# Two transformer layers with experts on one core: the transfer of the maxima's rows moved to ScalarE's queue, rounds of 31 and 23 blocks, and another build-time order

## The reference, cut to what matters

```
xn = layernorm(x)
x  = x + attention0(xn) + (routed0(xn) + shared(xn))     # layer 0
xn = layernorm(x)
x  = x + attention1(xn) + routed1(xn)                    # layer 1
```

## Time and profile before

| | |
|---|---|
| median of 3 runs | 691.94 us (689.86 to 697.47) |
| the profiled execution's own time | 687.82 us |
| its span, first to last instruction | 686.0 us |
| mean granted PE clock in it | 0.973 |
| PE, PEld, DVE busy | 643.7, 352.8, 502.2 us |
| ACT, POOL busy | 450.7, 308.7 us |

### The profile page before, as it was taken

How to read it: one execution, slowest core, us unless ns; L and a number is a source line. 1 busy time by engine, 2 the same in 40 slices (tenths; PEclk the granted TensorE clock), 3 DMA queues, 4 the chain that set the end, 5 groups by cost and what they waited for, 6 DMA issues and landing times.

```text
span 686.0 us, 13133 instructions
## 1 busy us (share of the span) xinstructions
PE 643.7 (94%) x4200; PEld 352.8 (51%) x4200; DVE 502.2 (73%) x1088; ACT 450.7 (66%) x843; POOL 308.7 (45%) x422
## 2 busy tenths in 40 slices
PE   2999987999999999898999999899999999999986
PEld 1876742654544454333466566555656555656221
DVE  3699779787778798777858777876677777666732
ACT  2443258777768878565877676666667667666774
POOL 3256844873155635646482122666365122122550
PEclk9999998999999999799999999899999999999997
DMA  8954216365344434336645444444755554431110
GB/s 232 295 151 146 84 50 184 118 202 158 103 134 135 149 118 127 102 90 197 212 118 175 146 152 132 145 144 141 219 182 164 161 164 134 140 93 37 47 48 16
DMA packets 82965, 95.16 MB, mean 139 GB/s; under 512 B 7249, under 2 KB 70097, under 8 KB 82897
## 3 DMA queue, kind: packets, MB, share of 16 engines
q1 hardware_dynamic: 78800, 85.91, 41.7%
q0 software_dynamic: 4096, 8.40, 4.2%
HBM read 67.68 MB, written 26.21 MB: 137 GB/s over the span
## 4 chain that ended last, share of the span: by engine, by line
PE 75%; DVE 9%; issue 4%; DMA 3%; POOL 3%; ACT 3%; SPq 2%; another core or an unknown queue 1%; POOLq 0%; DVEq 0%; ACTq 0%
PE pv_ps L917 15%; PE slot L888 15%; PE slot L905 13%; PE slot L865 9%; PE slot L878 6%; PE pv_ps L779 5%; DVE mx L1285 3%; PE slot L854 2%; PE slot L925 2%; PE slot L847 2%; DMA wbuf<-in_experts 1%; PE slot L790 1%; PE slot L897 1%; ACT probsT L1047 1%
## 5 line engine op out<-in xcount | busy, mean ns | idle before, releaser
L1285 DVE TENSOR_REDUCE mx<-slot 128x1 f32<-128x512 f32 x512 | 334.9, 685 | 117.7 <-PE slot L888 94.3
L1047 ACT ACTIVATE probsT<-slot 128x512 f32<-128x512 f32 x512 | 284.2, 597 | 90.4 <-PE slot L905 71.7
L888 PE MATMUL slot<-k_stack,q_stack 72*128 72x512 bf16 x512 | 197.9, 387 | 9.6 <-DVE mx L1285 7.9
L905 PE MATMUL slot<-q_stack,k_stack 75*128 75x512 bf16 x512 | 194.6, 390 | 9.4 <-issue 3.6
L917 PE MATMUL pv_ps<-probsT,v 128*32 128x512 f32 x1024 | 140.5, 621 | 0.9 <-ACT probsT L1047 0.8
L1379 POOL TENSOR_TENSOR hid<-th,up 128x512 f32<-128x512 f32 (+2 forms) x56 | 71.2, 1271 | 130.5 <-DVE th L1148 76.6
L888 PEld LDWEIGHTS slot<-k_stack,q_stack 72*128 72x128 bf16 x512 | 50.1, 98 | 131.8 <-issue 74.7
L1367 POOL DMA_INDIRECT yg<-ys_hbm,index x64 | 62.2, 972 | 45.5 <-issue 34.1
L865 PEld LDWEIGHTS slot<-xgT,wbuf 128*128 128x128 f32 (+1 forms) x576 | 75.6, 186 | 12.3 <-issue 1.1
L905 PEld LDWEIGHTS slot<-q_stack,k_stack 75*128 75x128 bf16 x512 | 50.2, 99 | 58.0 <-issue 19.0
L1356 POOL DMA_INDIRECT xs_hbm<-xn,index x64 | 64.0, 1000 | 32.4 <-DVE index L1262 16.4
(11 more groups left out here) (133 smaller groups left out, 605.5 us busy)
## 6 DMA issues: line engine op xcount, KB each, us to landing
wbuf<-in_experts SPq DMA_DIRECT2D x48, 544.0 KB, 4.9
q_stack<-parts_hbm SPq DMA_DIRECT2D x96, 96.0 KB
k_stack<-parts_hbm SPq DMA_DIRECT2D x96, 96.0 KB
wbuf<-in_experts SPq DMA_DIRECT2D x64, 128.0 KB, 2.7
xg<-xs_hbm SPq DMA_DIRECT2D x28, 256.0 KB
ys_hbm<-ys SPq DMA_DIRECT2D x28, 256.0 KB, 2.6
parts_hbm<-parts SPq DMA_DIRECT2D x16, 384.0 KB
xs_hbm<-zeros SPq DMA_DIRECT2D x2, 2048.0 KB, 12.6
```

The costliest lines, as they stand in the source:

```text
L888: nc.tensor.matmul(ps[:, 0:N], q_stack[0:STACK, h, j * P:(j + 1) * P], k_stack[0:STACK, h, :], start=True, stop=True).then_inc(slot_full, 1)
L905: nc.tensor.matmul(ps[:, 0:N], k_stack[0:STACK + MAXROWS, h, j * P:(j + 1) * P], q_stack[:, h, :], start=True, stop=True).then_inc(slot_fu ...
L1047: nc.scalar.activation(probsT[:, k % PROBS, a, :], ps[:, 0:N], ACT.Exp, scale=SCALE).then_inc(slot_free, 1)
L1285: nc.vector.tensor_reduce(mx[:, g, u // J, u % J:u % J + 1], ps[:, 0:N], AXIS.X, ALU.max)\
```

## The change

1. The DMA of the maxima's rows is no longer a part of SP's list. A new stage NW, on ACT, waits for ACT's own copy to `mxT` and issues the same DMA from ACT's queue. It has the wanted moment of NT, and the planner books 0.75 us of ACT for it.
2. A round has 31 and 23 blocks in place of 32 and 24. The last group of each round then has three blocks: `live(r, q)` says how many, and every stage of the group is cut to that many blocks of 128 columns.
3. Nearly all wanted moments are others, WARM goes from 196 to 169, and `EDGE` shifts the moments of M, MP, NT and of E, PV of eleven single groups.

```diff
-NB = (32, 24)
+NB = (31, 23)
...
-SETUP = (2.045, -9.522, 8.07, 1.095, -8.469, -2.988, -1.684, 25.862)
-ROUTE = (0.046, 0.046, 31.138, 28.95)
-WEIGH = 0.485
-GROUPS = ((4.838, 0.586), (17.79, 0.521), (16.756, 0.924), (29.504, 0.606))
-SLACK = 0.253
-LAG = {'RF': (2.324, -1.184), 'M': (-1.1, -0.238), 'MP': (0.506, 0.56), 'NT': (0.625, -0.823), 'E': (1.07, 3.793), 'PV': (0.552, 0.573), 'PO': (4.67, 1.118), 'AT': (23.765, 0.84), 'WL': (-0.359, -0.605), 'XL': (-0.911, 0.582), 'GG': (-0.389, 5.152), 'DN': (0.742, -0.665), 'YS': (0.607, -1.125), 'YG': (-0.253, 1.108), 'RK': (0.014, 2.373), 'SL': (-1.025, 0.721), 'HI': (17.634, 0.832), 'PW': (5.769, -0.579)}
-WARM = 196
...
+SETUP = (-0.46, -1.532, 5.793, 3.492, -23.822, 0.878, 1.105, 12.168)
+ROUTE = (0.886, 14.043, 38.797, 27.291)
+WEIGH = -0.398
+GROUPS = ((12.343, 0.126), (22.692, 0.887), (31.727, 4.574), (54.836, 0.664))
+SLACK = 0.345
+LAG = {'RF': (23.695, -0.259), 'M': (-21.601, -4.266), 'MP': (-0.425, 1.142), 'NT': (0.685, 0.935), 'E': (7.873, 0.784), 'PV': (0.501, 1.616), 'PO': (-1.379, -0.462), 'AT': (21.887, 9.677), 'WL': (-18.538, -1.787), 'XL': (1.939, 0.99), 'GG': (2.258, 0.12), 'DN': (1.136, 0.696), 'YS': (0.671, -2.158), 'YG': (-6.421, 0.417), 'RK': (-14.371, 21.752), 'SL': (-21.114, 15.903), 'HI': (11.067, 0.945), 'PW': (0.847, 0.172)}
+WARM = 169
...
+            m, e = EDGE.get("%d.%d" % (A, g), (0.0, 0.0))
             for u in range(HG * J):
-                put(t + LAG["M"][l] + u / 16, "M", A, g, u)
-            put(t + LAG["MP"][l], "MP", A, g)
-            put(t + LAG["NT"][l], "NT", A, g)
+                put(t + m + LAG["M"][l] + u / 16, "M", A, g, u)
+            put(t + m + LAG["MP"][l], "MP", A, g)
+            put(t + m + LAG["NT"][l], "NT", A, g)
+            put(t + m + LAG["NT"][l], "NW", A, g)
...
+def live(r, q):
+
+    return min(4, NB[r // 2] - 4 * q)
...
-            add(sp, ("NT", A, g), 0.75, 3.2, (act, ("NT", A, g)), chain="NT")
+            add(act, ("NW", A, g), 0.75, 3.2, (act, ("NT", A, g)), chain="NT")
...
-                elif kind == "NT":
-                    A, g = stage[1:]
-                    sp.wait_ge(*emptied(stage))
-                    sp.dma_start(q_stack[STACK:STACK + MAXROWS, g * HG:(g + 1) * HG, :], mxT[:, g % 2, :])\
-                      .then_inc(mx_in[g], 16)
...
-                    for b in range(4):
+                    for b in range(live(r, q)):
...
+                elif kind == "NW":
+                    A, g = stage[1:]
+                    sc.wait_ge(*emptied(("NT", A, g)))
+                    nc.scalar.dma_start(q_stack[STACK:STACK + MAXROWS, g * HG:(g + 1) * HG, :], mxT[:, g % 2, :])\
+                      .then_inc(mx_in[g], 16)
```

More of the change, by code:

```diff
@@ L131, in moments @@
             t = GROUPS[r][0] + GROUPS[r][1] * q
-            for b in range(4 * q, 4 * q + 4):
+            for b in range(4 * q, 4 * q + live(r, q)):
                 put(t + LAG["WL"][l], "WL", r, b)
@@ L298, in tasks @@
             k2 = ((k - 2) // G, (k - 2) % G)
-            add(act, ("NT", A, g), 0.5, 0.65, (pe, ("NT", A, g)), k >= 2 and (sp, ("NT", *k2)), chain="NT")
-            add(sp, ("NT", A, g), 0.75, 3.2, (act, ("NT", A, g)), chain="NT")
+            add(act, ("NT", A, g), 0.5, 0.65, (pe, ("NT", A, g)), k >= 2 and (act, ("NW", *k2)), chain="NT")
+            add(act, ("NW", A, g), 0.75, 3.2, (act, ("NT", A, g)), chain="NT")
             for j in range(J):
@@ L379, in tasks @@
             for part in (stage, up):
-                add(pe, part, 0.92, 1.2, (act, ("XG", r, q)), (sp, ("WL", r, 4 * q + 3)), chain="gated")
+                add(pe, part, 0.23 * live(r, q), 0.3 * live(r, q), (act, ("XG", r, q)), (sp, ("WL", r, 4 * q + live(r, q) - 1)), chain="gated")
         add(act, stage, 0.5 if up else 1.0, 0.66 if up else 1.2, (pe, stage), *free, chain="gated")
@@ L851, in _ @@
                     pe.wait_ge(*emptied(("XG", r, q)))
-                    pe.wait_ge(w_in[r][q], 64)
-                    for b in range(4):
+                    pe.wait_ge(w_in[r][q], 16 * live(r, q))
+                    for b in range(live(r, q)):
                         last = nc.tensor.matmul(ps[:, b * P:(b + 1) * P], wbuf[0][:, buffer_of(r, 4 * q + b), 0:P],
@@ L1003, in _ @@
                         sc.wait_ge(h_done, n - 1)
-                    nc.scalar.activation(th[0:rows, n % 2, :], ps[0:rows, 0:N], ACT.Tanh, scale=0.5)\
+                    w = N if kind == "SG" else live(*stage[1:3]) * P
+                    nc.scalar.activation(th[0:rows, n % 2, 0:w], ps[0:rows, 0:w], ACT.Tanh, scale=0.5)\
                         .then_inc(th_done, 1)
@@ L1011, in _ @@
                         sc.wait_ge(h_done, n - 1)
-                    nc.scalar.activation(up[0:rows, n % 2, :], ps[0:rows, 0:N], ACT.Copy, scale=0.5)\
+                    w = N if kind == "SU" else live(*stage[1:3]) * P
+                    nc.scalar.activation(up[0:rows, n % 2, 0:w], ps[0:rows, 0:w], ACT.Copy, scale=0.5)\
                         .then_inc(slot_free, 1)
@@ L1147, in _ @@
                     ve.wait_ge(*filled(source))
-                    nc.vector.scalar_tensor_tensor(out=th[0:rows, n % 2, :], in0=th[0:rows, n % 2, :], scalar=1.0,
-                                                   in1=slot[plan.ring[source]][0:rows, 0:N], op0=ALU.add, op1=ALU.mult)\
+                    w = N if source[0] == "SG" else live(*source[1:3]) * P
+                    nc.vector.scalar_tensor_tensor(out=th[0:rows, n % 2, 0:w], in0=th[0:rows, n % 2, 0:w], scalar=1.0,
+                                                   in1=slot[plan.ring[source]][0:rows, 0:w], op0=ALU.add, op1=ALU.mult)\
                         .then_inc(free_of(source), 1)
@@ L1378, in _ @@
                         gp.wait_ge(*filled(plan.down_of(n - HIDS)))
-                    nc.gpsimd.tensor_tensor(hid[0:rows, n % HIDS, :], th[0:rows, n % 2, :], up[0:rows, n % 2, :], ALU.mult)\
+                    w = N if source[0] == "SG" else live(*source[1:3]) * P
+                    nc.gpsimd.tensor_tensor(hid[0:rows, n % HIDS, 0:w], th[0:rows, n % 2, 0:w], up[0:rows, n % 2, 0:w],
+                                            ALU.mult)\
                         .then_inc(h_done, 1)
```

32 lines of the change are left out of this document (18 added, 14 removed).

## The result

The changed kernel took 708.5 us in the median of 4 runs (704.4 to 712.1), the kernel before 690.9 on the same chip: a ratio of 1.024, with a 95% interval of 1.014 to 1.034. That is slower by 17.6 us, where 682 was forecast and the range ended at 702. The profiled execution took 710.6 us, its span 708.8, at a mean granted clock of 0.958.

What follows compares the result with a forecast made beforehand. PE was taken to bound the middle (488 of 500 us), the chain set-up and DVE the start. Blocks -5.5, queue +2 and order -6 gave -9.5 on 691.9: 682 us, forecast's own range 676 to 688, full range 665 to 702.

Steps and rivals of the forecast that it cites:

- Blocks, -5.5 us: One block fewer per round: 22 expert products and four turns less on PE, -5.5 us, between -3 and -6.
- Queue, +2 us: Issuing the maxima's rows from ACT's queue: no gain on SP, 26.7 us of ACT, about one in fifteen reaching PE.
- Order, -6 us: New wanted moments, M before everything ready: first PV sooner at the start, -6 us, ends -26 and +13.
- the filler's price: WARM cut from 196 to 169: at least 25 stages of two zero matmuls fewer before the first PV, 5.5 us.
- +13 as the worst end: Slow end of the order's term, taken from the rival in which round 3 of the experts ends last.
- The premise under it: Half clock, 37 us over the whole kernel, follows PE standing still for DVE or ACT; 18 us if PE bound there.
- only the blocks count: Rival: order only moves waits and ACT's issues take back what it gives; 686.4 us, range 685 to 692, chance 0.18.
- The chain runs well ahead: Rival: 13 us at the start, 5.5 of blocks, 7 of half clock gained; 666 us, 658 to 676, chance 0.17.
- Round 3 of the experts: Rival: its groups come behind every E, so gathers, sums and output end the kernel; 703 us, 697 to 708, chance 0.13.
- the 657 of the condition: Last `ys` copy at the kernel's end: free up to 657 us, past it each us costs one.
- ACT paying for the queue: Rival: PE short of ACT at 24 of 32 issues, 20 us lost, no gain of order; 706 us, chance 0.07.
- Too little filler: Rival: first PV no sooner, so 5.5 us of PE open at the start, costing at most 3.4; 690 us, chance 0.07.

Runs made afterwards that it cites:

- second chip: Follow-up chip: kernel before 666.8 and 665.9 us in two groups of runs, changed kernel unaltered 659.9 us, ratio 0.992.
- first measurement: The changed kernel unaltered against the kernel before, as first timed: 708.5 us against 690.9, ratio 1.024.
- first chip: The chip on which the changed kernel was first timed against the kernel before: 708.5 us against 690.9, ratio 1.024.
- plain transfers: GpSimd's 64 scatters and 64 gathers made non-indirect, to or from consecutive rows, in either kernel: kernel before 665.7 us, changed kernel 658.1 us.
- fourth chip: Follow-up chip where indirect DMAs were replaced in both kernels; unaltered there, kernel before 691.3 us, changed kernel 711.4 us (one run).

## Why the prediction was wrong, step by step

**Blocks, -5.5 us.** The records are as counted: 24 fewer on line 870, 16 on 883, 4 on 852 and 4 on the layer-0 products. On the second chip the matmuls of lines 870 and 883 went from 76.9 + 51.0 to 72.9 + 50.7 us, 4.3 less; the rest of the 5.5 are turns and layer-0 products. No experiment isolates what reached the end, since the one with the blocks alone also had other lists and was 2.0 us slower, so the -5.5 itself is not shown.

**Queue, +2 us.** The row on ACT's queue is 0.73 us instead of 0.83. Kept in its lists the kernel before pays 4.5 us for the move, the changed kernel 1.7 or nothing. The size was of the right order and the argument stands: SyncE's queue cost nothing, and gain came from nowhere. (SyncE's issue follows the copy at once in 21 of the 32 groups, not in 20 as I wrote.) Who waited for an exponential in the changed kernel, first measurement:

```profile
  PEld slot L910: 18.4, 29
...
  PEld slot L893: 4.4, 7
  PEld pv_ps L922: 4.0, 6
```

That is 42 times and 26.8 us where the earlier trace rows has 34 times and 18.2: 8.6 us more, less than the 12 that I had named as a sign of a fault, though the 42 times are just over the 40 that I allowed. The rule that I quoted from the Trainium skill ("DMA: Bandwidth & Descriptors", section "Issuing engines are not separate DMA queues") agrees with the runs that moved this DMA alone: 670.4 against 665.9, 659.9 against 658.2 and 711.4 against 711.8 us, no gain in any beyond its spread.

**Order, -6 us. This step failed.** "I take -6 us, near the filler's price", with +13 as the worst end; measured, the term was about +21 us on the first chip. The first PV came at 88.8 us, 4.4 sooner, not quite the 88 that I asked for; on the second chip it was 86.6 against 87.7, so only about 1 of those 4.4 is there without late completions; the rest is what these cost the old kernel's start. With plain transfers on the fourth chip it is no sooner at all, 88.3 against 87.9. The hand-over of group 0, where the earlier trace rows has 75.07 to 82.79, in the changed kernel:

```profile
75.77 0.28 POOL L1404 TENSOR_SCALAR mx_neg<-mx 128x16 f32<-128x16 f32 x1 [0.34 <-issue]
...
80.93 0.59 ACT L1049 ACTIVATE mxT<-slot 12x512 bf16<-12x512 bf16 x1 [9.98 <-PE slot L902]
81.55 1.34 ACTq L1054 DMA_DIRECT2D q_stack<-mxT  x1
84.29 0.10 PEld L910 LDWEIGHTS slot<-q_stack,k_stack 75*128 75x128 bf16 x1
```

POOL took up the first maxima at 75.8 us, not before 70: M first did not pull it forward: the sixteen reductions start from 49.9 to 74.9 us, where the kernel before has them from 51.9 to 72.7, and 17.2 us of DVE's other work stands between them instead of 12.8. Where no start is late the whole change nevertheless gives 6.0 us (second chip) or 7.5 (plain transfers), against 9.5 forecast. Where they are late, the new lists lose: the indirect transfers cost them 53.3 us and the old ones 25.7, by the fourth chip. So the step did not fail by its arithmetic on the filler: the sum had no term at all for waits beside the indirect DMAs, which on the first chip became 25 late starts in the new lists, 49.8 us, where the old ones had 14 and 25.0. With -5.5 and +2 left as they are, the order's term was about -3 on the one sort of chip (-2.5 and -4.0) and about +21 on the other. Since the -5.5 was not isolated, the -3 is a remainder and may be less.

**The premise under it.** I read the pieces at half clock as following "stretches in which PE stood still for want of DVE or ACT", and went no further. The piece from 284 to 294 stood in front of me: it lies within round 2's scatters (277 to 316 us), and 0.50 of clock over 10 us needed a reason. (The slices of the earlier trace rows hid it: those of lower clock hold thinner work of PE themselves, but at 17 and 26 the slice before is at 9, so my word that they follow thinner ones is right for the start and the end alone.) Asking why DVE and ACT stood would have shown waits that no engine ended, eight of them in the trace of before, up to 4.4 us long, beside GpSimd's scatters and gathers. A list that is tuned or judged without them says little of one that must live with them. That would not have given the sign, but it would have given a rival with a place, a price (20 us and more at stake in either direction) and a condition.

**Rivals.** On a chip without late starts the 6.0 and 7.5 us are as near to *only the blocks count*, 5.5, as to the forecast's 9.5. *The chain runs well ahead* is out: the first PV is 4.4 us sooner at most and the end later. Round 3 of the experts did end late: the last `ys` copy at 656.9 is just at the 657 of the condition, and gathers run to 689.4. Yet it is no cause: everything slid by 22 us, E's own last group with it, and from the last `ys` copy to the end there are 51.9 us against 51.7 before. The changed time falls near the time that this rival gave, 703, for another reason. ACT paying for the queue is excluded by the run that moved the DMA back (711.8). Too little filler: the start was level, 84.4 against 83.0 us at the first E, and stayed so.

**What the new lists have that makes late completions dear** is argued and not shown. Each M and E fills a slot that only DVE or ACT can empty, on a signal from PE; an expert's product needs fewer such signals for its time. In the seven stretches of scatters and gathers after the first one, each from its first issue to the end of its last, the new lists have PE at 598 matmuls other than M, E and PV, the old ones at 674. In the two of rounds 2 and 3 of scatters the new lists had 27.3 us at half clock and 9.0 us of PE's idle time, the old ones 13.2 and 3.0. That fits, but no run moved expert products into those stretches, and on the second chip, where nothing is lost, the two counts differ too (613 and 676).

## What to carry to other kernels

Before costing a new order, look at what ended the long waits and the pieces at half clock of the old one; a wait that no instruction ended, with two engines starting together behind it, is not slack that an order can take back, and may be the thing that decides. Compare one list with another on more than one chip: here a 0.8% gain and a 2 to 3% loss were both measured well, of the same two kernels. And parts of a planned order can't be tried one by one with the planner running: hold the lists, or what is compared is another list.

## What the runs showed of the hardware that was not expected

On all chips but the second, DVE and ACT started a reduction or an exponential 0.6 to 4.2 us after its matmul had ended and they were free, on the first chip 14 times in the kernel before (25.0 us), on three chips 25 to 27 times in the changed one (43.0 to 51.5 us), each within 1 us of GpSimd's issues of indirect DMAs; on the second chip not once in either. With plain transfers of the same bytes by the same queue there was none, on a chip where the unaltered changed kernel had 27. Indirect transfers are worth 25.7 us of 691 there in one list and 53.3 us of 711 in another. On the same chips the trace also lacks some 90 to 110 of 1432 records of PE's semaphore rises, so that the time to the next recorded rise overstates how many signals are late (158 to 206 of PE's in a full kernel; 3 to 7 on the second chip). What differs between the chips, and by what path an indirect DMA holds up the signals, no run here shows. And a pause of ScalarE can cost more than it lasts: 35.8 us of added copies made one kernel 57.6 us slower, with 119 us of its trace at half clock.
